# A cross-attention and mixture-of-experts layer on one core: fewer waits on gathers and scatters, the last tiles' outputs and the last root moved, the setup reordered

## The reference

```
x = x + xattn(layernorm(x), ctx)
x = x + ffn(layernorm(x))

xattn(x, y):                     # 16 heads of 16
  y_dca, y_main = y[:, -16:], y[:, :-16]
  k_dca = ln(y_dca @ Wk_dca + b) * w + b;  v_dca = y_dca @ Wv_dca + b
  q = ln(x @ Wq + bq) * w + b;  k = ln(y_main @ Wk + bk) * w + b;  v = y_main @ Wv + bv
  return (softmax(q k' / 4) v + softmax(q k_dca' / 4) v_dca) @ Wo + bo

ffn(h):                          # 4096 rows, 16 experts, 2 of them for each row
  s = sigmoid(h @ router); choose the best 2 experts of the best 2 of 4 groups, by s + e_bias
  weights = the two s, divided by their sum
  routed = sum over the two experts e: weight_e * (relu(h @ up[e])^2 @ down[e])
  return routed + relu(h @ shared_up)^2 @ shared_down
```

## Time and profile before

| | |
|---|---|
| median of 3 runs | 504.17 us (501.42 to 505.55) |
| the profiled execution | 506.52 us |
| its span | 504.8 us |
| PE busy | 469.1 us, 93% |
| DVE, ACT, POOL busy | 340.5, 299.8, 308.0 us |
| scatters, 64 | 63.4 us of POOL, 990 ns each |
| gathers, 64 | 61.6 us of POOL |
| moved | 82.91 MB, mean 164 GB/s |

### The profile page before, as it was taken

One profiled execution on the slowest core, in us unless ns is written; L12 is line 12 of the kernel. 1 busy time (PEld: TensorE's weight loads), 2 busy tenths in 40 slices (PEclk: granted clock), 3 DMA queues, 4 the chain that ended last, 5 costly groups with the idle time before them and its releaser, 6 DMA issues.

```text
span 504.8 us, 14776 instructions
## 1 busy us (share of the span) xinstructions
PE 469.1 (93%) x5631; PEld 376.9 (75%) x5631; DVE 340.5 (67%) x801; ACT 299.8 (59%) x583; POOL 308.0 (61%) x490
## 2 busy tenths in 40 slices
PE   7968899999999999999889999989999999999981
PEld 6556787788887788888666676869999999756671
DVE  4885886788898899898976677614444455574343
ACT  2477676678777777878646543256665756352500
POOL 7358786766677687767423666756640366646751
PEclk9999999999999999999979999999999999999997
DMA  7221223132233331212246899478998899886343
GB/s 201 72 59 55 69 81 101 47 94 89 79 102 100 101 92 46 74 56 82 73 138 199 283 324 367 178 243 295 301 312 260 283 301 336 275 270 198 95 120 119
DMA packets 88232, 82.91 MB, mean 164 GB/s; under 512 B 22098, under 2 KB 80868, under 8 KB 88164
## 3 DMA queue, kind: packets, MB, share of 16 engines
q1 hardware_dynamic: 80724, 63.88, 40.5%
q0 software_dynamic: 6144, 16.79, 10.0%
q10 hardware_dynamic: 1296, 1.31, 1.0%
HBM read 38.96 MB, written 41.94 MB: 160 GB/s over the span
## 4 chain that ended last, share of the span: by engine, by line
PE 42%; POOL 4%; issue 3%; DMA 3%; ACT 2%; DVE 2%; another core or an unknown queue 1%; POOLq 0%; DVEq 0%; ACTq 0%
PE ps L1544 10%; PE ps L1552 8%; PE ps L1654 7%; PE ps L1666 6%; PE ps L1641 3%; POOL kdT L873 1%; PE ps L1417 1%; POOL XN L873 1%; DMA XN<-slot_x 1%; PE ps L1440 1%; PE ps L1401 1%; DMA slot_x<-XN,slot_i 1%; POOL slot_x L846 1%; PE ps L1381 1%
## 5 line engine op out<-in xcount | busy, mean ns | idle before, releaser
L846 POOL DMA_INDIRECT slot_x<-XN,slot_i x64 | 63.4, 990 | 32.5 <-issue 13.7
L1552 PE MATMUL ps<-sd_sb,hid 128*128 128x256 f32 x256 | 57.7, 381 | 1.5 <-issue 1.5
L1544 PE MATMUL ps<-xT_ch,su_sb 128*128 128x512 f32 x128 | 58.6, 603 | 0.2 <-ACT probsT L888 0.2
L1552 PEld LDWEIGHTS ps<-sd_sb,hid 128*128 128x128 f32 x256 | 48.2, 190 | 11.6 <-issue 5.6
L873 POOL DMA_INDIRECT XN<-slot_y,slot_i x40 | 38.6, 966 | 26.2 <-issue 13.2
L2057 DVE COPY ey<-ps 128x512 f32<-128x512 f32 x48 | 30.8, 685 | 30.1 <-PE ps L1666 17.5
L1007 ACT ACTIVATE relu<-ps 128x512 f32<-128x512 f32 x32 | 19.0, 594 | 46.7 <-PE ps L1544 46.1
L1666 PE MATMUL ps<-down_sb,ea 128*128 x188 | 44.6, 380 | 0.7 <-issue 0.7
L1654 PEld LDWEIGHTS ps<-XN,tile_w 128*128 128x128 f32 x376 | 43.8, 192 | 0.8 <-issue 0.2
L1654 PE MATMUL ps<-XN,tile_w 128*128 128x128 f32 x376 | 44.0, 275 | 0.0
L1784 DVE TENSOR_REDUCE pmax<-ps 128x16 f32<-128x768 f32 x64 | 41.0, 682 | 3.8 <-PE ps L1381 3.5
(11 more groups left out here) (241 smaller groups left out, 1065.1 us busy)
## 6 DMA issues: line engine op xcount, KB each, us to landing
XN<-slot_x SPq DMA_DIRECT2D x24, 512.0 KB
slot_y<-ey SPq DMA_DIRECT2D x24, 512.0 KB
slot_x<-zeros SPq DMA_DIRECT2D x16, 384.0 KB, 3.3
slot_x<-zeros SPq DMA_DIRECT2D x4, 1536.0 KB
x_in<-in_x SPq DMA_DIRECT2D x16, 256.0 KB, 3.2
xn2T_dram<-xn2T SPq DMA_DIRECT2D x16, 256.0 KB
xT_ch<-xn2T_dram SPq DMA_DIRECT2D x16, 256.0 KB
out<-X SPq DMA_DIRECT2D x15, 256.0 KB
```

The costliest lines, as they stand in the source:

```text
L846: pool.indirect_dma_start(slot_x[:, :], bass.IndirectOffsetOnAxis(ap=slot_i[:, k, t:t + 1], axis=0), XN2[:, t, :], None).then_inc(s_scat[t ...
L1544: last = pe.matmul(up_bank(c, m), su_sb[:, k, m * P:(m + 1) * P], xT_ch[:, c % 2, k, :], start=(k == 0), stop=(k == KC - 1))
L1552: last = pe.matmul(shared_out(c, t), hid[:, c % 2, m, t * P:(t + 1) * P], sd_sb[:, m, :], start=(m == 0), stop=(m == NM - 1))
```

## The change

It has five parts.

1. Setup: on PE one `dca_kv` goes ahead of `transpose_vectors`, and `bias_through_wo` ahead of the extra keys' transposes, which now stand together ahead of `transpose_q(0)`. On POOL the Newton step of the extra keys (`dca_roots`) is a function of its own; for the first half it goes ahead of `normalise_q(0)`, for the second behind the first `dca_blocks`, ahead of the step's `newton_roots`. ACT and DVE follow in their order.
2. The last `newton_roots`, among the scatters on POOL, becomes `last_roots` on DVE, for two columns and not 68.
3. `scatter_pace` has 4 marks ahead of the experts where it had 11, and its regular part begins at scatter 36 and takes five steps, where it began at 40 and took four. `gather_pace` loses all its marks of the tail but one, at 48.
4. The outputs of the last half step (three tiles that can be in use) are copied and stored by ACT; the fourth, unused tile of `slot_y` is zeroed by SP beforehand.
5. DVE adds chunk 6 of the shared part ahead of the last `combine`.

```
@@ SP @@
+                if i == GROUPS + 1:
+                    sp.dma_start(slot_y[P * (SLOT_TILES - 1):P * SLOT_TILES, :], zeros[:, :]).then_inc(s_zero[1], 16)
...
             def store_tiles(i):
-                for h in range(2):
+                for h in range(2 if i + 1 < STEPS else 1):
@@ POOL, step(i) @@
+                if i == 1:
+                    dca_roots(0)
+                    dca_normalise(0)
                 if active(i - 1):
                     normalise_q(i - 1)
-                    if i < 3:
-                        dca_normalise(i - 1)
                     if i == 2:
+                        dca_normalise(1)
                         add_bo(0)
...
                     dca_blocks(i - 1)
+                    if i == 1:
+                        dca_roots(1)
@@ POOL, marks @@
-            scatter_pace = {8: (s_u_ps, 9), 12: (s_u_ps, 10), 16: (s_dr, 4), 20: (s_d_ps, 2), 24: (s_u_ps, 15), 28: (s_dr, 8),
-                            32: (s_dr, 10), 35: (s_dr, 12), 37: (s_u_ps, 18), 38: (s_eT_ps, 1), 39: (s_d_ps, 4)}
-            for i in range(4):
-                n = 40 + 6 * i
+            scatter_pace = {14: (s_u_ps, 10), 24: (s_u_ps, 14), 32: (s_eT_ps, 1), 34: (s_eT_ps, 2)}
+            for i in range(5):
+                n = 36 + 6 * i
                 scatter_pace[n] = (s_h_ps, 2 * i + 1)
                 scatter_pace[n + 1] = (s_h_ps, 2 * i + 2)
                 scatter_pace[n + 2] = (s_eT_ps, 2 * i + 3)
                 scatter_pace[n + 3] = (s_y_ps, 2 * i + 1)
                 scatter_pace[n + 4] = (s_eT_ps, 2 * i + 4)
                 scatter_pace[n + 5] = (s_y_ps, 2 * i + 2)
-            gather_pace = {36: (s_dr, 13), 40: (s_d_ps, 5), 44: (s_u_ps, 27), 48: (s_dr, 17), 52: (s_u_ps, 29),
-                           56: (s_u_ps, 32), 60: (s_dr, 21)}
+            gather_pace = {48: (s_u_ps, 26)}
...
-            for n in range(4):
-                scatter(n)
-            newton_roots(GROUPS + 2)
-            for n in range(4, 2 * TT):
+            for n in range(2 * TT):
                 scatter(n)
@@ ACT, behind the last expert step @@
+            act.wait_ge(s_y_ps, 2 * STEPS)
+            act.wait_ge(s_ys[1], 16 * (STEPS - 1))
+            evac(ey[:, 1, 0:2, :], ffn_bank[6].rearrange("p (j d) -> p j d", j=2)).then_inc(s_yl, 1)
+            evac(ey[:, 1, 2, :], ffn_bank[7][:, 0:D]).then_inc(s_yl, 1)
+            act.wait_ge(s_yl, 2)
+            row = P * UNROLL * (2 * STEPS - 1)
+            act.dma_start(slot_y[row:row + 3 * P, :].rearrange("(j p) d -> p j d", p=P), ey[:, 1, 0:3, :]).then_inc(s_ys[1], 16)
@@ PE @@
             project_k(1)
+            dca_kv(0)
             transpose_vectors()
...
             transpose_k(0)
-            transpose_dca_k(range(0, 1))
+            bias_through_wo()
+            transpose_dca_k(range(0, 2))
             transpose_q(0)
-            transpose_dca_k(range(1, 2))
-            bias_through_wo()
@@ DVE @@
             sigmoid(GROUPS - 3)
+            last_roots()
             tile_table(0, ch_first)
...
-            for u in range(13, UNITS):
+            for u in range(13, UNITS - 1):
                 combine(u)
+            shared_add(6)
+            combine(UNITS - 1)
             dve.wait_ge(s_used, UNITS)
-            shared_add(6)
```

More of the change, by code:

```diff
@@ L1107, in _ @@
                 .then_inc(s_col, 1)
-            square_q(0)
+            copy_dca_v(0)
             root_seeds(0)
-            for n in range(DT):
+            for n in range(1, DT - 1):
                 copy_dca_v(n)
             square_dca(0)
+            copy_dca_v(DT - 1)
             dca_seeds(0)
@@ L1120, in _ @@
             act.wait_ge(s_col, 1)
-            copy_dca_kT(range(0, 1))
+            copy_dca_kT(range(0, 2))
             copy_qT(0)
-            copy_dca_kT(range(1, 2))
             square_q(1)
@@ L1577, in _ @@
             project_k(1)
+            dca_kv(0)
             transpose_vectors()
-            for n in range(DT):
+            for n in range(1, DT):
                 dca_kv(n)
@@ L2115, in _ @@
             gather_vars(0)
+            dca_k(0)
             head_vars(0)
-            for n in range(DT):
+            for n in range(1, DT):
                 dca_k(n)
@@ L2123, in _ @@
             dve.tensor_scalar(k_b2[:, :], half[:, :], ln_col[:, 3:4], None, ALU.mult).then_inc(s_prep, 1)
-            for n in range(DT, DT + 2):
+            for n in range(DT, 2 * DT):
                 dca_k(n)
             head_vars(1, (0,))
-            for n in range(DT + 2, 2 * DT):
-                dca_k(n)
+            x_stats(2)
+            dve.wait_ge(s_bo_ps, 1)
+            dve.tensor_tensor(bo_sb[:, :], bank[7][:, 0:D], bo_sb[:, :], ALU.add).then_inc(s_bo, 1)
             copy_q(1)
-            x_stats(2)
             gather_vars(1)
```

32 lines of the change are left out of this document (26 added, 6 removed).

## The result

The changed kernel took 511.04, 513.67, 511.24 and 525.91 us, a median of 512.45, beside 503.75 for the kernel before. Some executions of any kernel fall into a slower state with a lower clock, as the last of the four did, and all ratios, here and in the experiments, are of the other executions, called the counted runs. The ratio is 1.0166, 95% interval [1.0102, 1.023]. I had forecast 500.4 with a range to 505.5, so the forecast was wrong in sign. The profiled execution took 511.04 with a span of 509.3, 4.5 more than the 504.8 of before.

The account below looks back on a forecast made before the run. The prediction took PE to bound the kernel, except where it waits or has ended. From the median, 504.17 − 0.9 (setup) − 1.6 (first-half marks) + 2.7 (second-half marks) − 4.0 (tail) = 500.4 us, range 496.0 to 505.5.

Parts of the forecast that it names:

- What bounds the kernel: Whole kernel: an edit pays where PE waits or after PE has ended; a faster engine beside busy PE pays nothing.
- Last Newton step: Among the first scatters: six operations move from POOL to DVE, hidden by DVE's 4.58 us idle; worth nothing on PE.
- Marks on the scatters, first half: Ahead of the experts: fewer marks start scatter 31 at 319.3, not 323.95, so tile loads come sooner; gain 1.6 us.
- The forecast of the waits: Start of the experts: PE's 1.15 us wait before the first tile transposes goes; the 1.36 us one may go.
- Second half: Seventh expert step: last scatter waits for a later product, so tile loads are late; loss 2.7 us (1.3 to 6.1).
- Rival D: Seventh step: a wait over 3.6 us drops PE's clock to half, making the kernel slower, 507.2 us; chance 0.08.
- my own list of signs: Forecast is wrong if the seventh-step wait is nil or above 5, half clock follows, or the final chain uses POOL.
- The loss of 1.7: Seventh step: estimate from the skill's transfer times, 2.3 us a scatter and 3.2 a load; whole kernel 499.4 us.
- Setup: Setup: bias products fill PE's wait for the extra keys, first scores at 32.1, not 32.97; gain 0.9 us (0 to 1.2).
- Tail: After the experts: earlier stores and unmarked gathers let PE end the chain; gain 6.4 us by trace, 4.0 against the median.
- Rival E: Tail doesn't move, as packed gathers slow one another or stores land no sooner: 504.4 us; chance 0.05.
- Shifts ahead of the experts add up: Gains or losses ahead of the experts carry to the end, because PE is nearly full behind them; no size given.

Follow-up runs that it names:

- e4: Kernel before with the new tail alone (ACT's output copies and stores, chunk 6 earlier, one gather mark); fast chip, 0.9909 of the kernel before.
- e1: Changed kernel with the whole scatter table of before; fast chip, 0.9973 of the kernel before.
- e13: Changed kernel with the second half's scatter marks of before and the last Newton step back on POOL behind the fourth scatter; slow chip, 0.9934 of the kernel before.
- e2: Changed kernel with the six first-half scatter marks of before (8 to 28) in place of 14 and 24; fast chip, 0.9947 of the kernel before.
- e3: Changed kernel with the setup of before on all engines; fast chip, 0.9969 of the kernel before.
- e5: Changed kernel as it is, measured again on the fast chip; 0.9988 of the kernel before.
- e7: Kernel before with only the new scatter table and the last Newton step on DVE; fast chip, 1.0067 of the kernel before.
- e9: Changed kernel as it is, measured again on a slow chip; 1.006 of the kernel before.
- e12: Changed kernel with all scatter marks of before, last Newton step still on DVE; slow chip, 0.9824 of the kernel before.
- e18: Changed kernel with all scatter marks of before, on another slow chip; 0.9918 of the kernel before.
- e6: Changed kernel with the scatter marks of before from 32 on, keeping 14 and 24; fast chip, 0.9873 of the kernel before.
- e14: Kernel before with the new setup and the new tail, scatter marks and Newton step as before; slow chip, 0.9887 of the kernel before.
- e16: Changed kernel with the second half's scatter marks of before and one more mark, at scatter 8; slow chip, 0.9946 of the kernel before.
- e10: Changed kernel with the scatter marks of before from 32 on, keeping 14 and 24; slow chip, 0.9955 of the kernel before.
- e11: Changed kernel with the regular scatter marks begun at 38 in place of 36 and ended at number 63; slow chip, 1.0078 of the kernel before.
- e15: Changed kernel as it is, measured again on another slow chip; 1.0108 of the kernel before.
- e17: Changed kernel with the scatter marks of before from 32 on, no mark at 8; slow chip, 0.9991 of the kernel before.
- e8: Kernel before, unchanged, run once on a slow chip for its profile; no ratio given.

## Why the prediction was wrong

*What bounds the kernel.* Right: an edit pays or costs where PE waits. I read it as "an engine that gets faster beside a busy PE pays nothing", and left out that it can cost: POOL got faster, and PE lost 6.5 us.

*Last Newton step, "by itself worth nothing on PE".* On F its move is worth 0.7 (B of e4 against e1). On a slow chip it also removes the pause that parted the first scatters (e13). I priced its instructions and not its place in POOL's queue.

*Marks on the scatters, first half: gain 1.6.* This is the step that failed. The forecast of the waits was right (none ahead of the first tile transposes), but number 31 started at 325.47 and not at 319.3, because everything had slid by the stall: A rose by 6.5, and by 6.5 to 9.6 in all six profiles with the run of 14 away from chip F. Even on F the marks gave nothing: B is 42.92 with the old marks (e1) and the new. The error was to price a transfer's start on POOL alone, with no term for what a run of them does to PE's signals. Nothing that I gave excluded a loss, so the bound below should have been open.

*Second half: loss 2.7 (1.3 to 6.1).* The mechanism was as told: mark, last scatter at 383.64, loads at 386.53, PE's wait. From the last scatter's start to the load were 2.9 us and from the load to PE's start 3.9, less than the 4.69 and 5.44 of before, so the low end that I took was right. The wait was 2.14 to 2.8 (forecast 1.6 to 6.4), but with the half clock C rose by 3.5 in the first pair and by 4.2 to 4.7 in e2, e3 and e5 against 7.90. Rival D had this mechanism and a wrong threshold: I read 3.6 us from what followed the last product, and here the clock fell behind waits of 2.14 to 2.75 in six profiles, and in e7 after 2.40 not at all. The row named showed when it fell once, not the least wait that suffices. By my own list of signs, half clock behind this wait, the forecast is wrong here too. The loss of 1.7 that I put beside the sum as an estimate doesn't follow from its figures: transfers of 2.3 and 3.2 us end at 383.5 to 385.2, a wait of 0.1 to 1.8 and a loss of at most 1.5. The Trainium skill (TensorE: Matmul & The Clock Gate, HAM oscillation — how this bites in real kernels) tells of a wait for DMA after which PE works cold; e5's windows agree, 0.51 behind the wait.

*Setup: gain 0.9.* The first scores stood at 31.81, near the forecast 32.1. Then PE's clock was at half from about 32 to 39 (mean 0.93 in the setup's window), and the gain was gone. The ratios of e3 and e5 can't tell such a difference. Open.

*Tail: 6.4 against this trace, 4.0 against the median.* D fell by 4.0 in the first pair, by 3.2 to 4.2 on F (e7's 65.5 against 61.3 to 62.3) and by 3 to 5 on slow chips (71.9 and 72.3 against 67 to 69). e9's 76.3 is the exception: there PE pauses twelve times between 485 and 505, up to 1.51 us at once, and why is open. The lower of my two numbers was right, also for the profiled run. Rival E falls.

*"Shifts ahead of the experts add up".* The stall did carry through: no later stretch gave it back.

Together, from the first pair: −4.0 tail, +6.5 run of scatters, +3.5 seventh step, +2.15 in the first five steps, −0.4 in B, make 7.8. The 2.15 are small waits for ACT's copies. They appear in all slow-chip profiles to some degree, and their cause stays open.

**A version that beats both:** the changed kernel with all scatter marks of before (e1, e12, e18). It was below the kernel before on each chip: 0.9973, 0.9824 (three counted runs) and 0.9918, where only the last two intervals exclude 1. On chip F e6 stood lower (0.9873, four counted runs), with the same stretches. The surest single part is the new tail: alone (e4, 0.9909) and with the new setup (e14, 0.9887) its intervals exclude 1.

## What to carry to other kernels

A wait in the queue of an engine that issues transfers may be what keeps the other engines' signals on time: before one is removed, or work beside the transfers moved away, count how many transfers will then follow one another, mark which signals of the other engines fall late into that run and are waited for, and give the sum a term for it, open upwards. A new pause can move such a stall instead of removing it (e16), so follow the runs to the end of the stage. Read a profile of the kernel before as one chip's: here the same change was even on one chip and 0.6 to 1.7% slower in the three other measurements (the interval of one of them reaches below 1), so a forecast of under 1% needs its chip. And price a new wait of PE with the half clock that may follow: behind the setup, eleven waits of 2.05 to 2.75 us had it at their end or behind them, and one of 2.40 had not.

## What the runs showed of the hardware

**PE's signals wait for the end of a run of scatters, on some chips.** In the six slow-chip profiles with 14 in a row beside the last transposes (the first, e9, e10, e11, e15, e17), the signal of the last transposes came 6.9 to 7.8 us after their end and 1.8 to 2.5 us after POOL had finished issuing the 14th scatter (290.50 and 292.28 in the first trace, 293.82 and 296.35 in e15, by the semaphore's updates in the trace). Shorter and longer runs there did it too: seven in e11, eight in e8 (each 1.6 us from the last scatter's end to the signal), 16 in e16 (3.2 us). Early in a run the signals were in time, as in e13 three scatters into its ten. On F, with the same 14, it came at once. ACT's timeline of e15, then of e5:

```profile
296.16 0.20 ACT L1000 ACTIVATE sig<-ps 128x32 f32<-128x32 f32 x1 [8.97 <-remote]
```

```profile
288.56 0.60 ACT L895 ACTIVATE xn2T<-ps 128x512 f32<-128x512 f32 x1 [0.91 <-PE ps L1466]
```

A full DMA alone doesn't explain it: the window of e15 from the last transposes to the last scatter has a DMA share of 0.54, though that of e16's 16 scatters is full (1.04).

```profile
289.00:292.70 3.70, 0.48 (x5) 0.25 (x3) 0.68 (x4) 0.00 (x0) 2.88 (x3) 1.00 0.54 186
```

The Trainium skill (Perfetto Trace Analysis, in its table for the Tensor engine) has a matmul's signal go out once PSUM has acknowledged the write, and calls the profiled end an estimate. No run here shows which link is held up, the write or the signal, nor why chip F is free of it. That it is the scatters' run, and not something that happens beside it, rests on e12, e13, e16 and e18 against e10 and e17, and on e8 and e16, where the late signals stand at the end of another run.

**The clock also falls to half behind shorter waits, in some executions.** Spells of 3.4 or 6.8 us stand inside full stretches of PE too, at other places in each run. e1 had one in the attention loop, with a wait of 1.09 us ahead of it:

```profile
168.00 0.81 PE L1433 MATMUL ps<-v_rows,probsT 64*64 64x34 f32 x37 [1.09 <-issue]
168.60:172.00 3.40, 3.40 (x49) 2.43 (x42) 2.65 (x7) 1.66 (x4) 2.35 (x4) 0.50 0.52 134
```

Between 46 and 270 us the 20 profiles have 21 such spells, that of the earlier trace rows among them, and 20 of them began in or up to 2.4 us behind a wait of PE of 1.0 to 2.3 us in the same products (`v_rows`), which ended by nothing that the profile shows. Seven waits there were of 1.75 us or more, all with a spell; 16 of 0.95 to 1.4 us had none, so the shorter ones don't decide it alone. What makes these waits is open. e7 has one of 1.12 us and no spell up to its tail. On F the time rises by 5.9 us for each 0.01 by which the run's mean clock is lower (a straight line through its 136 runs, with a level for each kernel in each set), which is most of the spread from 484 to 504 us.
